# Attention scores of a two-layer graph network: 24 products of 32-row strips per tile on unpadded q and k, in place of 6 full products on zero-padded ones

## The reference

```python
# layer 0 (adj masks: -9e15 where adj <= 0), layer 1 (adj as a bias, no mask)
q = split_heads(x @ Wq + bq)                       # layer 1 has no bq, bk
k = split_heads(x @ Wk + bk)
v = split_heads(x @ Wv + bv)
scores = einsum('bhqd,bhkd->bhqk', q, k) * SCALE   # per graph and head: 64 x 64, over 32 features
scores = scores + beta * adj                       # layer 1: scores + adj
probs = softmax(scores, axis=-1)
out = einsum('bhqk,bhkd->bhqd', probs, v)          # layer 1: then @ Wo.T + bo
x = layernorm(x + out)
```

## Time and profile before

| | |
|---|---|
| time, median of 3 runs | 1205.56 us (1204.38 to 1207.96) |
| span of the profiled execution | 1204.9 us |
| PE busy | 1134.8 us, 94% of the span |
| DVE busy | 955.2 us, 79% |
| ACT busy | 595.5 us, 49% |
| POOL busy | 531.1 us, 44% |

### The profile page before, as it was taken

How to read it: one execution, slowest core, us unless ns; L and a number is a source line. 1 busy time by engine, 2 the same in 40 slices (tenths; PEclk the granted TensorE clock), 3 DMA queues, 4 the chain that set the end, 5 groups by cost and what they waited for, 6 DMA issues and landing times.

```text
span 1204.9 us, 30454 instructions
## 1 busy us (share of the span) xinstructions
PE 1134.8 (94%) x12288; PEld 1002.0 (83%) x12288; DVE 955.2 (79%) x1662; ACT 595.5 (49%) x904; POOL 531.1 (44%) x454
## 2 busy tenths in 40 slices
PE   5799999999989999899998999989999999999876
PEld 3688888889878888788887888878888889898765
DVE  5747978798877988679796797968879797886945
ACT  5355455554545545355552555535555554545331
POOL 0324545444443544445453354533545454454622
PEclk9899999999999999899998999989999999999987
DMA  8020212111020210202001021200212102011000
GB/s 256 6 71 1 70 30 63 30 27 56 23 71 30 62 30 8 71 29 63 30 27 59 23 63 37 62 17 24 69 30 63 30 14 69 23 35 30 15 14 27
DMA packets 61666, 52.96 MB, mean 44 GB/s; under 512 B 35920, under 2 KB 55376, under 8 KB 61520
## 3 DMA queue, kind: packets, MB, share of 16 engines
q1 hardware_dynamic: 60320, 49.10, 13.6%
q10 hardware_dynamic: 1200, 1.77, 0.4%
HBM read 38.28 MB, written 12.58 MB: 42 GB/s over the span
## 4 chain that ended last, share of the span: by engine, by line
PE 88%; DVE 4%; issue 4%; ACT 1%; POOL 1%; DMA 1%; SPq 0%; POOLq 0%; DVEq 0%; ACTq 0%
PE ps_u L372 48%; PE ps_s L385 16%; PE ps_o L372 8%; PE ps_p L447 7%; PE ps_p L461 7%; PE ps_x L399 2%; PE ps_o L475 2%; DVE row_sum L700 1%; DMA q_par<-in_wk 1%; DVE probs L654 1%; DVE row_max L663 1%; DVE xt_lo L680 0%; POOL probs L793 0%; POOL probs L799 0%; ACT q_par L555 0%
## 5 line engine op out<-in xcount | busy, mean ns | idle before, releaser
L793 POOL TENSOR_TENSOR probs<-probs,row_max 128x768 f32<-128x768 f32 x128 | 209.4, 1636 | 379.8 <-DVE row_max L663 379.8
L799 POOL TENSOR_TENSOR probs<-probs,row_inv 128x768 f32<-128x768 f32 x128 | 190.6, 1489 | 136.2 <-DVE row_inv L708 72.1
L555 ACT ACTIVATE q_par<-ps_u,q_bias,q_scale 128x512 f32<-128x512 f32 x192 | 139.2, 775 | 205.1 <-PE ps_u L372 203.2
L385 PE MATMUL ps_s<-k_blk,q_par 128*128 128x128 f32 x1536 | 212.9, 290 | 24.0 <-issue 20.8
L385 PEld LDWEIGHTS ps_s<-k_blk,q_par 128*128 128x128 f32 x1536 | 188.6, 198 | 36.6 <-issue 22.2
L534 ACT COPY probs_t<-ps_p 128x768 f32<-128x768 f32 x128 | 102.5, 801 | 161.0 <-PE ps_p L447 161.0
L700 DVE TENSOR_REDUCE row_sum<-probs 128x12 f32<-128x768 f32 x128 | 121.7, 950 | 34.0 <-ACT probs L571 32.7
L562 ACT ACTIVATE k_blk<-ps_u,k_bias 64x512 f32<-64x512 f32 x192 | 130.7, 681 | 33.1 <-PE ps_u L372 31.5
L372 PE MATMUL ps_u<-w_hi_v,xt_lo 128*128 128x384 f32 x384 | 137.8, 359 | 0.0
L372 PE MATMUL ps_u<-xt_hi,w_lo_q 128*128 128x512 f32 x288 | 124.3, 432 | 11.9 <-DVE w_lo_q L639 11.6
L812 POOL TENSOR_TENSOR rstd<-var_eps,minus_half 128x1 f32<-128x1 f32 x128 | 70.3, 549 | 144.8 <-DVE var_eps L744 144.8
(11 more groups left out here) (68 smaller groups left out, 2116.6 us busy)
## 6 DMA issues: line engine op xcount, KB each, us to landing
xt_in<-in_x_t SPq DMA_DIRECT2D x16, 768.0 KB, 6.6
x_in<-in_x SPq DMA_DIRECT2D x16, 768.0 KB, 4.6
out<-z SPq DMA_DIRECT2D x64, 192.0 KB, 1.9
adj<-in_adj SPq DMA_DIRECT2D x64, 128.0 KB, 4.3
q_par<-in_wq ACTq DMA_DIRECT2D x1, 576.0 KB, 6.5
q_par<-in_wk ACTq DMA_DIRECT2D x1, 576.0 KB, 8.7
v_sb<-in_wv ACTq DMA_DIRECT2D x1, 576.0 KB, 12.7
q_par<-in_wq SPq DMA_DIRECT2D x1, 576.0 KB, 10.6
```

Source lines behind the costliest of these rows:

```text
L385: last = nc.tensor.matmul(ps_s[:, b, 2 * g * NODES:(2 * g + 2) * NODES], q_par[layer][:, g, GT * t + b, :, :], k_blk[layer][:, g, GT * t + ...
L555: done = nc.scalar.activation(q_par[layer][:, g, :, par, :], src.rearrange("p (b n) -> p b n", b=GC), ACT.Identity, bias=q_bias[layer][:, ...
L793: nc.gpsimd.tensor_tensor(s, s, over_keys(row_max[p]), ALU.subtract).then_inc(shifted, 1)
L799: nc.gpsimd.tensor_tensor(s, s, over_keys(row_inv[p]), ALU.mult).then_inc(probs_ready, 1)
```

## The change

q and k are kept once each, unpadded (`q_sb`, `k_sb`, half the size). `scores` makes, for each of 3 feature groups, 2 graphs and 4 heads, a product of its own: 32 rows, 64 stationary columns (q), 64 moving columns (k). The four heads of a group lie on rows 0, 32, 64 and 96; they write partitions 0 to 63, 64 to 127, 0 to 63 and 64 to 127 of `ps_s`, the first two in its first bank, the other two in its second. ACT evacuates a unit with one instruction of 128x512 in place of two. The bias is added with another order of `ps_s` (same elements), and `heads` reads `probs_t` in the matching order. The zero masks, their constants and the memsets of `k_blk` go.

```diff
@@ buffers
-        q_par = [sb(f"q_par{l}", [P, KT, GC, 2, NODES]) for l in range(2)]
-
-        k_blk = [sb(f"k_blk{l}", [P, KT, GC, 2, NODES]) for l in range(2)]
+        q_sb = [sb(f"q_sb{l}", [P, KT, GC, NODES]) for l in range(2)]
+        k_sb = [sb(f"k_sb{l}", [P, KT, GC, NODES]) for l in range(2)]
...
@@ scores (PE)
-                for b in range(GT):
-                    for g in range(KT):
-
-                        last = nc.tensor.matmul(
-                            ps_s[:, b, 2 * g * NODES:(2 * g + 2) * NODES],
-                            q_par[layer][:, g, GT * t + b, :, :],
-                            k_blk[layer][:, g, GT * t + b, :, :], start=True, stop=True)
+                for g in range(KT):
+                    for b in range(GT):
+                        for hh in range(HG):
+                            rows = slice(hh * HD, (hh + 1) * HD)
+                            half_of, par = hh // 2, hh % 2
+                            at_key = (g * GT + b) * NODES
+                            last = nc.tensor.matmul(
+                                ps_s[par * NODES:(par + 1) * NODES, half_of, at_key:at_key + NODES],
+                                q_sb[layer][rows, g, GT * t + b, :],
+                                k_sb[layer][rows, g, GT * t + b, :], start=True, stop=True)
                 last.then_inc(scores_made, 1)
@@ heads (PE)
-                                probs_t[keys, h // 2, (h % 2) * NODES:(h % 2 + 1) * NODES],
+                                probs_t[keys, half_of * KT + g, par * NODES:(par + 1) * NODES],
@@ unit_out (ACT)
-                if kind == "q":
-                    for par in range(2):
-                        done = nc.scalar.activation(q_par[layer][:, g, :, par, :],
-                                                    src.rearrange("p (b n) -> p b n", b=GC), ACT.Identity,
-                                                    bias=q_bias[layer][:, g, par:par + 1],
-                                                    scale=q_scale[layer][:, par:par + 1])
+                dst = (q_sb if kind == "q" else k_sb)[layer][:, g, :, :].rearrange("p b n -> p (b n)")
+                if layer == 0 and kind == "q":
+                    done = nc.scalar.activation(dst, src, ACT.Identity, bias=q_bias[:, g:g + 1], scale=SCALE[0])
+                elif layer == 0:
+                    done = nc.scalar.activation(dst, src, ACT.Identity, bias=k_bias[:, g:g + 1])
+                elif kind == "q":
+                    done = nc.scalar.mul(dst, src, SCALE[1])
                 else:
-                    for blk in range(2):
-                        rows = slice(blk * 2 * HD, (blk + 1) * 2 * HD)
-                        done = nc.scalar.activation(k_blk[layer][rows, g, :, blk, :],
-                                                    src[rows, :].rearrange("p (b n) -> p b n", b=GC),
-                                                    ACT.Identity, bias=k_bias[layer][rows, g:g + 1])
+                    done = nc.scalar.copy(dst, src)
@@ start and bias_and_max (DVE)
-            for l in range(2):
-                nc.vector.memset(k_blk[l][:].rearrange("p g b j n -> p (g b j n)"), 0.0).then_inc(const_set, 1)
...
                 nc.vector.tensor_tensor(
-                    s[:], ps_s[:, :, 0:PAIRS * NODES].rearrange("p b (i k) -> p i b k", i=PAIRS),
-                    bias[:, GT * t:GT * t + GT, :].unsqueeze(1).to_broadcast([P, PAIRS, GT, NODES]),
+                    s[:].rearrange("p (a g) b k -> p a g (b k)", a=2),
+                    ps_s[:, :, 0:KT * keys].rearrange("p a (g n) -> p a g n", g=KT),
+                    bias[:, GT * t:GT * t + GT, :].rearrange("p b k -> p (b k)").unsqueeze(1).unsqueeze(1)
+                    .to_broadcast([P, 2, KT, keys]),
                     ALU.add).then_inc(biased, 1)
```

More of the change, by code:

```diff
@@ L146, in two_gnn_layers_kernel @@
         bq_col = sb("bq_col", [P, KT])
-        q_scale = [sb(f"q_scale{l}", [P, 2]) for l in range(2)]
-        q_bias = [sb(f"q_bias{l}", [P, KT, 2]) for l in range(2)]
-        k_bias = [sb(f"k_bias{l}", [P, KT]) for l in range(2)]
+        q_bias = sb("q_bias", [P, KT])
+        k_bias = sb("k_bias", [P, KT])
         minus_half = sb("minus_half", [P, 1])
@@ L218, in two_gnn_layers_kernel @@
         stage = {"v0": v_sb[1][:, 0:KT, :], "v1": x1[0][:, 0:KT, :], "o1": x1[1][:, 0:KT, :]}
-        q_flat = [q_par[l][:].rearrange("p g b h n -> p (g b h n)") for l in range(2)]
-        for n, (l, k) in {"q0": (0, 0), "k0": (0, 1), "q1": (1, 0), "k1": (1, 1)}.items():
-            stage[n] = q_flat[l][:, k * KT * D:(k + 1) * KT * D].rearrange("p (g n) -> p g n", g=KT)
+        for n, home in {"q0": q_sb[0], "k0": k_sb[0], "q1": q_sb[1], "k1": k_sb[1]}.items():
+            flat = home[:].rearrange("p g b n -> p (g b n)")
+            stage[n] = flat[:, 0:KT * D].rearrange("p (g n) -> p g n", g=KT)
         def phase(step, attend=None, behind=None, turn_x=None, project=None, unit_steps=UNITS_OF_STEP,
@@ L330, in _ @@
             sp.dma_start(bq_col[:], bq0).then_inc(small_in, 16)
-            sp.dma_start(k_bias[0][:], bk0).then_inc(small_in, 16)
+            sp.dma_start(k_bias[:], bk0).then_inc(small_in, 16)
             sp.dma_start(beta_col[:], beta.rearrange("(o n) -> o n", o=1).partition_broadcast(P))\
@@ L603, in _ @@
         def _(dve):
-            for l in range(2):
[L606 to L613, removed]
-                nc.vector.memset(k_blk[l][:].rearrange("p g b j n -> p (g b j n)"), 0.0).then_inc(const_set, 1)
-            n_set = 2 * HG * 2 + 4
             def constants():
-                dve.wait_ge(const_set, n_set)
                 dve.wait_ge(small_in, 16 * 6)
[L620 to L623, removed]
+                nc.vector.tensor_scalar(q_bias[:], bq_col[:], SCALE[0], None, ALU.mult).then_inc(const_set, 1)
+                dve.wait_ge(const_set, 1)
                 nc.vector.memset(minus_half[:], -0.5).then_inc(const_ready, 1)
@@ L653, in bias_and_max @@
                 s = probs[t % 2]
+                keys = GT * NODES
                 nc.vector.tensor_tensor(
-                    s[:], ps_s[:, :, 0:PAIRS * NODES].rearrange("p b (i k) -> p i b k", i=PAIRS),
-                    bias[:, GT * t:GT * t + GT, :].unsqueeze(1).to_broadcast([P, PAIRS, GT, NODES]),
+                    s[:].rearrange("p (a g) b k -> p a g (b k)", a=2),
+                    ps_s[:, :, 0:KT * keys].rearrange("p a (g n) -> p a g n", g=KT),
+                    bias[:, GT * t:GT * t + GT, :].rearrange("p b k -> p (b k)").unsqueeze(1).unsqueeze(1)
+                    .to_broadcast([P, 2, KT, keys]),
                     ALU.add).then_inc(biased, 1)
@@ L739, in residual @@
                 nc.vector.bn_stats(stats[p][:], z[p][:]).then_inc(stats_ready, 1)
-                dve.wait_ge(const_set, n_set + 2)
+                dve.wait_ge(const_set, 1)
                 dve.wait_ge(stats_ready, at(tile) + 1)
```

## The result

The changed kernel takes **1139.9 us** (median of 4 runs, 1138.1 to 1142.9) against 1205.1 us: ratio 0.9463, 95% interval 0.9443 to 0.9483, 65 us less. The prediction said 1155 (1130 to 1215).

A forecast was written before the change was run, and what follows sets the result against it. PE's stream was taken to bound the steady loop. 1205.6 less 49.3 (shorter scores in 112 tiles), 0.5 (ACT's evacuations) and 0.4 (earlier start) gave 1155.4 us, with a range from 1130 to 1215.

The forecast's parts named there:

- What bounds: Steady loop: PE never idle, so a microsecond taken from its stream is one of the kernel, until DVE binds.
- The stage: Scores on PE: from 1.40 to 0.96 us per tile, a saving of 0.44 us per tile.
- all four places always streaming: Lower bound for the strips' scores stage: 12 x 57 ns per place, 0.78 us to the next kind of product.
- used no better than in `heads`: Upper bound for the scores stage: half as many places as `heads`, 2 x 0.50 + 0.15 = 1.15 us.
- 7 of 8 tiles: PE's wait for a phase's tight tile hides one tile's saving in eight; 112 x 0.44 = 49.3 us arrive.
- The rest: Outside the scores stage: 0.5 us from ACT's evacuations (0 to 5.9 possible), 0.4 from an earlier start.
- Instructions: PE's fetching of 33,792 records in place of 24,576, seen at the loop's back edge: at worst +8 us, priced at 0.
- Turns at a bank: Rival, scores: strips writing the same bank of `ps_s` run two at a time; +8 us, 1213 us; chance 0.13.
- Loads not hidden within a strip: Rival, scores: weight loads add to each strip's stream, 12 x (57 + 61) ns; +14, 1220 us; chance 0.08.
- No overlap: Rival, scores: strips run one after another, 2.83 us per tile; 1389 us; chance 0.05.
- DVE as the bound: Rival, loop: DVE binds in half the steps, so only 28 us arrive; 1177 us; chance 0.12.

The follow-up runs named there:

- strips_padded: Changed kernel's strips, but reading the padded q and k of before, with two evacuations per unit and the memsets: 1144.5 us against 1204.1, ratio 0.9501.
- half_moving: Changed kernel with 32 moving columns (keys) in each strip product, half of the scores left out: 1138.3 us, one execution, read for the stage alone.
- full_at_y0: strips_padded with 6 full products again in the first tile of each Y phase, 16 of 128 tiles: 1157.1 us, ratio 0.9610.
- full_at_y1: strips_padded with 6 full products again in the second tile of each Y phase, 16 of 128 tiles: 1163.4 us, ratio 0.9662.
- full_unpadded: Changed kernel with 6 full products of 128 rows per tile instead of strips, keeping unpadded buffers and single evacuations: 1198.7 us, ratio 0.9950.
- strips_twice: Changed kernel with all 24 strips of a tile computed twice, 96 records: 1281.9 us, ratio 1.065.
- halves_swapped: Changed kernel with bank and column half exchanged, so neighbouring strips share a column half instead of a bank: 1139.2 us, ratio 0.9455.
- same_place: Changed kernel with the same 24 strips, head outermost, so the six products of one row group follow each other: 1348.2 us, ratio 1.118.
- same_place_half: same_place with 32 of 64 keys (moving columns) in each product, the rest left out: 1384.6 us, one execution.

## Why the prediction was right, and where it was off

- **What bounds.** Right: PE's stream was the path, and what its stage lost the kernel lost. By the steps, 112 x (1.40 - 0.86) + 16 x 0.12 = 62 us, less 64 x 0.05 for slower transposes (below), is 59 us; `strips_padded` gained 60.
- **The stage**, the term that was mis-sized: 0.96 us taken, 0.86 measured. I took the middle between "all four places always streaming" (0.78) and "used no better than in `heads`" (1.15). The first was nearly exact: 12 records per place at 59 ns in place of 57. The second scaled an average, while in `heads` the first 22 records already started at 8 ns, that is 8 places at about 60 ns each; only its last third was slow. The reason given for the first was incomplete all the same: the 57 ns were read as the time of 64 moving columns, and `half_moving` shows that 32 take as long beside 64 stationary ones. The middle of two bounds stood for no mechanism; the strips behaved as at the lower one.
- **7 of 8 tiles.** Right, shown by `full_at_y0` and `full_at_y1`: 0.12 against 0.53 us.
- **The rest.** 0.9 us taken, with an upper bound of 5.9 + 0.5 = 6.4; `full_unpadded` gained 4 to 8. Three of them come from the start: the first scores start at 32.1 us in the kernel before and at 29.0 now. I had looked for what the evacuations cost in the steady loop, where it is nothing, and not at the first phases, where PE waits for each.
- **Instructions.** Priced at 0 with +8 as the worst; right here: the idle time at the back edge, at its first of four turns, went from 5.4 to 4.5 us. `strips_twice` shows that the next step of this kind would not be free: there PE stands for its instructions inside the strips.
- **Rivals.** Turns at a bank: excluded by the change's own 0.85 us and by `halves_swapped`. Loads not hidden within a strip: excluded by the pace of the change itself, 59 ns a record and not the 118 of load and stream one after the other. No overlap: it exists, in another order of the same products (`same_place`), so it was a question of the program's order and not of the chip alone. DVE as the bound: not reached, though near. Busy time in 100 us of the loop (PE, PEld, DVE, ACT, POOL, then the granted clock PEclk):

```profile
500.00:600.00 100.00, 99.61 (x1597) 86.31 (x1596) 91.36 (x158) 42.46 (x68) 50.85 (x43) 1.00 0.17 51
```

DVE works 91 of 100 us and PE is never long idle. The 1.83 us of slack of the earlier trace rows are 1.49 now, read at the same place of the loop: the scaling ends at 572.61 and the transposes start at 574.10.

```profile
571.14 1.47 POOL L787 TENSOR_TENSOR probs<-probs,row_inv 128x768 f32<-128x768 f32 x1 [0.57 <-DVE row_inv L692]
574.10 0.82 PE L448 MATMUL ps_p<-ident,probs 128*128 128x128 f32 x6
```

- What the Trainium skill says ("TensorEngine Tiling (Array Packing)", Gotcha 1: PSUM Pressure) of row tiles that share a bank did not show as time lost here, with disjoint partitions. Its section Instruction Overhead says that a matmul with one moving column takes as long as one with 60; in `half_moving` and `same_place_half` a record of 32 columns takes as long as one of 64, 58 to 59 ns, but the load of 64 stationary columns can be the reason, so these runs do not confirm it.

## What to carry to other kernels

Block-diagonal padding that makes many small products into a few full ones can be dearer than the small products, if these are issued so that neighbours lie on different row groups of the array. Count them by place: records on the fullest place times about 59 ns, plus 0.15 us for each change of the kind of product; halving the columns on one side alone bought nothing here, and both sides at once was not tried. The 59 ns are those of the full clock; at half of it they were 106. Keep the loop over the places innermost, and take such a count from the trace's nearest relative at full rate, not from its average.

## What the runs showed of the hardware

- **A pace per record and place.** At a granted clock of 1.00 it is 58 to 59 ns with 64 stationary columns, whether 64 or 32 columns move, and 56 ns with 32 stationary and 64 moving ones; at 0.50 it is 106 ns in all three.
- **Little overlap across places when one place's products stand together.** In `same_place` the 48 records take 2.25 us, the time of about 39 records one after another; so some nine are hidden, three at each change of the row group.
- **PE stands when its instructions come late.** The 53 stops inside the strips, in four kernels, end 1.2 to 1.6 us after a transfer of instructions on q8.
- **Transposes behind strips are slower.** Groups by line and form, the kernel before, then the changed one:

```profile
L399 PE MATMUL ps_x<-ident,x 128*128 128x128 f32 x192 | 31.5, 273 | 0.0
```

```profile
L400 PE MATMUL ps_x<-ident,x 128*128 128x128 f32 x192 | 34.8, 290 | 0.0
```

Three of them are 0.05 us longer; 64 times that is 3 us, a cost that the prediction did not have.

- **The clock fell while PE was busy.** In `same_place_half` the mean granted clock was 0.917, against 0.955 in `same_place` and 0.977 in the change. Three neighbouring stretches of it (PE, PEld, DVE, ACT, POOL, PEclk as above):

```profile
436.00:442.50 6.50, 6.50 (x118) 6.12 (x117) 4.71 (x10) 2.30 (x4) 2.30 (x3) 1.00 0.09 31
442.60:446.00 3.40, 3.40 (x16) 3.30 (x15) 3.37 (x5) 0.00 (x0) 1.64 (x1) 0.51 0.00 0
446.00:452.00 6.00, 6.00 (x115) 5.46 (x114) 4.36 (x11) 2.50 (x4) 2.02 (x2) 1.00 0.01 3
```

PE was busy in all of the first stretch, 2.4 us of it with small products one after another on one place; then it ran 3.4 us at the lower of its two levels, 1.2 GHz. In the change such stretches come only after the loop's back edge, at the start and at the end. This can explain why `same_place_half`, with the shorter stage, is the slower kernel by 36 us. As an estimate from the mean clocks, 0.917 over 1382.8 us against 0.955 over 1350.8 is some 108 us more at half clock, which costs at most 54 us; the shorter stages give 128 x 0.11 = 14 back.
